# Attention's ScalarE loop written out, and a block's sums copied out by VectorE

## The reference

```python
q = (x_norm @ Wq + bq).reshape(B, S, H, hd).transpose(0, 2, 1, 3)
k = (x_norm @ Wk + bk).reshape(B, S, H, hd).transpose(0, 2, 1, 3)
v = (x_norm @ Wv + bv).reshape(B, S, H, hd).transpose(0, 2, 1, 3)
q = apply_rope(q)
k = apply_rope(k)
q = q * (1.0 / jnp.sqrt(jnp.float32(hd)))
scores = jnp.einsum('bhqd,bhkd->bhqk', q, k)
attn = jax.nn.softmax(scores, axis=-1)
out = jnp.einsum('bhqk,bhkd->bhqd', attn, v)
```

## Time and profile before

| what | value |
|---|---|
| time, median of 3 runs | 4466.51 us (4465.53 to 4467.92) |
| the profiled execution's own time | 4463.72 us |
| its span in the trace | 4462.0 us |
| TensorE busy | 93% of the span |
| VectorE busy | 70% |
| ScalarE busy | 60% |
| attention, blocks 1 to 30 | about 805 to 3308 us of the span |

### The profile page before, as it was taken

One profiled execution on the slowest core, in us unless ns is written; L12 is line 12 of the kernel. 1 busy time (PEld: TensorE's weight loads), 2 busy tenths in 40 slices (PEclk: granted clock), 3 DMA queues, 4 the chain that ended last, 5 costly groups with the idle time before them and its releaser, 6 DMA issues. The chain is left out here.

```text
span 4462.0 us, 71502 instructions
## 1 busy us (share of the span) xinstructions
PE 4160.7 (93%) x23748; PEld 1788.7 (40%) x23748; DVE 3137.1 (70%) x4158; ACT 2665.3 (60%) x5113; POOL 374.6 (8%) x444
## 2 busy tenths in 40 slices
PE   6988637999999999999999999999998899999999
PEld 4666401222222222222222222222225788876666
DVE  6877596999999999999999999999950011132332
ACT  4555304778777778778778778778784222222122
POOL 0222355000000000000000000000001000011110
PEclk8999758999999999999999999999999999999999
DMA  4232393000004000004000000000004755532221
GB/s 149 76 104 90 113 152 116 6 4 4 6 4 73 12 4 4 6 4 72 14 4 4 6 4 4 6 4 4 6 4 161 230 193 195 198 100 73 64 60 40
DMA packets 206165, 264.69 MB, mean 59 GB/s; under 512 B 24880, under 2 KB 169520, under 8 KB 204240
## 3 DMA queue, kind: packets, MB, share of 16 engines
q1 hardware_dynamic: 193872, 228.98, 17.8%
q0 software_dynamic: 11904, 31.10, 2.4%
HBM read 184.76 MB, written 74.97 MB: 58 GB/s over the span
## 5 line engine op out<-in xcount | busy, mean ns | idle before, releaser
L1172 ACT ACTIVATE a_PT<-a_PS 128x512 f32<-128x512 f32 x4096 | 2119.2, 603 | 687.6 <-PE a_PS L1046 608.3
L1253 DVE TENSOR_REDUCE a_MX<-a_PS 128x2 f32<-128x1024 f32 x1062 | 1290.6, 1221 | 149.0 <-PE a_PS L1031 136.0
L1259 DVE TENSOR_REDUCE a_MX<-a_PS 128x1 f32<-128x512 f32 x1972 | 1266.7, 684 | 66.2 <-PE a_PS L1031 45.6
L1046 PE MATMUL a_PS<-a_QS,a_KS 128*128 128x512 bf16 x4096 | 1075.5, 383 | 24.2 <-ACT a_PT L1172 9.5
L1056 PE MATMUL a_OT<-a_PT,a_VG 128*32 128x512 f32 x8192 | 1095.2, 607 | 0.9 <-ACT a_PT L1172 0.8
L1031 PE MATMUL a_PS<-a_KS,a_QS 64*128 64x512 bf16 x4096 | 731.5, 393 | 111.5 <-ACT a_PT L1172 48.2
L1031 PEld LDWEIGHTS a_PS<-a_KS,a_QS 64*128 64x128 bf16 x4096 | 172.5, 93 | 1179.6 <-ACT a_PT L1172 639.7
L1046 PEld LDWEIGHTS a_PS<-a_QS,a_KS 128*128 128x128 bf16 x4096 | 314.1, 97 | 624.6 <-DVE a_MX L1253 281.3
L1444 ACT ACTIVATE e_hT<-e_up,e_BF 128x256 f32<-128x256 f32 x312 | 148.2, 475 | 413.3 <-PE e_up L1397 413.2
L1397 PE MATMUL e_up<-e_xT,e_WF 128*128 128x256 f32 x1248 | 324.7, 383 | 0.8 <-DVE e_xT L1454 0.8
L1406 PE MATMUL e_dn<-e_WP,e_hT 128*128 128x256 f32 x1248 | 322.0, 381 | 0.0
(11 more groups left out here) (222 smaller groups left out, 2783.4 us busy)
## 6 DMA issues: line engine op xcount, KB each, us to landing
e_WF<-Wfc SPq DMA_DIRECT2D x39, 1024.0 KB, 5.0
e_WP<-Wproj SPq DMA_DIRECT2D x39, 1024.0 KB, 7.0
a_QS<-scr_qparts SPq DMA_DIRECT2D x384, 32.0 KB, 9.5
a_KS<-scr_kparts SPq DMA_DIRECT2D x48, 256.0 KB, 13.3
scr_xs<-f_zero SPq DMA_DIRECT2D x1, 9984.0 KB, 33.2
e_XS<-scr_xs SPq DMA_DIRECT2D x39, 256.0 KB, 2.7
scr_ys<-e_Y SPq DMA_DIRECT2D x39, 256.0 KB, 2.1
f_X<-x SPq DMA_DIRECT2D x16, 512.0 KB, 4.7
```

Source lines behind the costliest of these rows:

```text
L1046: T.matmul(score_bank(c), KS[j][:, h, u * P:(u + 1) * P], QS[j][:, bass.ds((b * HG + h) * BLK, BLK)], start=True, stop=True).then_inc(S["q ...
L1172: nc.scalar.activation(PT[:, c % RING, :], score_bank(c), ACT.Exp, scale=SOFT_SCALE).then_inc(S["exp_done"], 1)
L1253: V.tensor_reduce(MX[n % 2][:, :, x], PS[:, banks[0]:banks[0] + SIDES, :], AX.X, ALU.max).then_inc(S["mp_free"], SIDES)
L1259: V.reduce_max(MX[n % 2][:, side, x:x + 1], PS[:, banks[side], :], AX.X).then_inc(S["mp_free"], 1)
```

## The change

ScalarE's `act.Fori` over the blocks becomes a Python loop, so its 31 passes stand one after the other in the stream, with constants for the counts that its waits compare with. The copy of `OT` to `OS` goes from ScalarE to VectorE: a new function `copy_out(n)` with the same two waits, called at the start of VectorE's block n+1, before pair 0, and once at the very end. The first increment of `o_copied`, which stands for the copy of a block that doesn't exist, moves along.

```diff
@@ nc.scalar of attention @@
             act.sem_inc(S["av_done"], KT)
-            act.sem_inc(S["o_copied"], 1)
...
                 if more:
                     for c in range(HG):
                         exp(n + 1, c)
-                act.wait_ge(S["av_done"], (n + 2) * KT)
-                act.wait_ge(S["att_store"], n * 16 + 1 + 16)
-                nc.scalar.copy(OS[:], OT[:]).then_inc(S["o_copied"], 1)
 
             for c in range(HG):
                 exp(0, c)
-            with act.Fori(0, NG * NB - 1) as n:
+            for n in range(NG * NB - 1):
                 one_block(n, True)
             one_block(NG * NB - 1, False)
@@ nc.vector of attention @@
             c = Chain(dve, S["chain"])
+            dve.sem_inc(S["o_copied"], 1)
...
+            def copy_out(n):
+
+                dve.wait_ge(S["av_done"], (n + 2) * KT)
+                dve.wait_ge(S["att_store"], n * 16 + 1 + 16)
+                V.tensor_copy(OS[:], OT[:]).then_inc(S["o_copied"], 1)
+
             def one_block(n, more1, more2):
                 e = first_event(n)
+                if n:
+                    copy_out(n - 1)
                 for x in range(PAIRS):
...
             for n in range(blocks):
                 one_block(n, n + 1 < blocks, n + 2 < blocks)
+            copy_out(blocks - 1)
```

## The result

The changed kernel takes 4424.9 us (median of 4, 4413.6 to 4428.0), the kernel before 4466.0 beside it: a ratio of 0.9904, interval 0.9885 to 0.9923. It was compared on three more occasions: 0.9920 (0.9906 to 0.9933), 0.9914 (0.9901 to 0.9926) and 0.9924 (0.9911 to 0.9938). By the medians it gains 41, 36, 38 and 36 us. The forecast was 33 us, 4433.8 us, in a range of 4426 to 4450.

A forecast was written before the change was run, and what follows sets the result against it. TensorE was taken as the bound, idle mainly at 30 block boundaries behind ScalarE's branch back. Removing 1.46 us and adding 0.37 for the copy, 30 times, gave 32.7 us less: 4433.8 us from 4466.5, range 4426 to 4450.

The forecast's parts named there:

- The stall and its cause: ScalarE's loop end: the branch back forces an instruction fetch, and TensorE waits 1.32 us for an exponential, 30 times.
- The 1.46 us of a boundary: Between blocks: period 83.63 us against 82.17 without a stall; writing the loop out removes it 30 times, 43.8 us.
- The copy's cost: Start of VectorE's block: the copy delays reductions 0.52 us, 0.15 absorbed, costing 0.37 us in each of 30 blocks.
- the overlap: VectorE: operations of 0.68 us start 0.60 us apart, so the next starts before the one before is done.
- The prediction's reading of the Trainium skill: VectorE: no start until the previous pipe is empty; 0.71 us delay, 0.56 us cost, total gain 27 us; not followed.
- The sum over the blocks: Boundaries of blocks 1 to 30: 30 x (1.46 - 0.37) = 32.7 us less.
- The copy on ScalarE: gain: Taking the 0.62 us copy off ScalarE gains nothing, since ScalarE has slack in a step.
- "some us" for block 0: Block 0, where GpSimd's scatter disturbs every engine: some us allowed within the forecast's own spread of 4428 to 4442.
- the range: Whole kernel: 4426 to 4450 us, meant to take in most of the costly-copy rival at 4450 us (chance 0.14).
- the register instructions: Between ScalarE's exponentials: removing them gains nothing, because TensorE doesn't wait for ScalarE inside a block.

The follow-up runs named there:

- e6: Kernel of before with two blocks in a pass of ScalarE's loop, 14 branches back instead of 30, copies still on ScalarE: 4416.5 us, ratio 0.9950.
- e1: Changed kernel with the copy of OT left on ScalarE, so only the loop is written out: 4413.9 us, ratio 0.9896.
- e5: Changed kernel with ScalarE's loop kept and a bare wait on ScalarE where the copy was: 4439.7 us, ratio 0.9997.
- e8: Changed kernel with each block's sums copied twice on VectorE, first into a tile nobody reads: 4427.3 us, ratio 0.9972.
- g3: Kernel of before with ScalarE's block 0 written out and blocks 1 to 30 in the loop: 4438.4 us, ratio 0.9995.
- g4: Kernel of before with ScalarE's loop written out except block 0, which stands in a loop of a single pass: 4395.2 us, ratio 0.9893.
- e2: Changed kernel with ScalarE's loop back, so only the copy is moved to VectorE: 4431.8 us, ratio 0.9930.
- f1: Kernel of before, unchanged, run again as first of four combinations of the change's two parts: 4459.8 us, ratio 1.0003.
- e7: Kernel of before, loop and ScalarE's copy kept, each pass cut 8 exponentials behind the copy: 4405.8 us, ratio 0.9919.

## Why the prediction missed

**The stall and its cause: right.** The gap belongs to the branch back and not to the `weigh` that the profile names. `e6` has stalls only at branches, `e1` has none, and `e5` brings them back by a wait ahead of the branch. The 1.46 us of a boundary were measured as 83.63 - 82.16 = 1.47.

**The copy's cost: right.** 0.37 us were forecast and 82.55 - 82.16 = 0.39 measured, and 0.38 of it lies in the five scores where the prediction looked for it. That a longer delay of the reductions would pass one to one isn't shown, since in `e8` the `weigh` waited for the copy itself. The copy started 1.14 us behind a reduction of 1.23, and the next operation 0.60 behind a copy of 0.68, so the overlap holds here. The prediction's reading of the Trainium skill (VectorE: DVE Perf Modes, section The DRAIN you can't avoid) would have made the cost 0.56. That reading took one sentence of the section alone; the same section says that a next operation that isn't held, as it calls it, starts earlier, and with that the trace agrees.

**The sum over the blocks: right.** From block 0's copy to block 30's it is 2507.0 us before and 2474.1 after, 32.9 less; 32.7 were forecast.

**"The copy on ScalarE: gain": wrong on its own, though not in the sum.** I gave the move nothing, since ScalarE has slack in a step. The copy's time does cost nothing, but its wait held the branch back by about 1.2 us, just enough to bring the fetch into TensorE's way. Moving the copy alone brings a block to 82.61 us against 82.55 with both parts, so in blocks 1 to 30 either part brings nearly all of the gain, and both together hardly more than one. Over the whole execution that doesn't hold: by the medians the copy alone gained 28 and 27 us, both parts 36 and 38 beside it, and the loop alone 46 and 48. What I called the price of a branch is the price of a branch taken late. `e5` shows it by a bare wait.

**Outside blocks 1 to 30: the step that failed.** The sum gave everything but the 30 boundaries nothing, with "some us" for block 0 inside the range, and said that the register instructions were worth nothing. In the profiled pair the spans differ by 40.8 us: 3.1 before attention's first sums, 3.3 in block 0, 32.9 from its copy to block 30's, and 1.5 behind that.

Of these, only block 0's part repeats. Where before takes some 4460 us, six profiles with ScalarE's loop and six with it written out have the first sums at 688.7 and 688.3 us by their means, and the rest behind block 30's copy lasts 1151.7 and 1152.5. Block 0 is 5.9 us shorter when written out, with hardly any overlap between the two sixes. So the term that was mis-sized is block 0's, and the other 4.6 us of the pair are, by the same profiles, chance of two executions.

By the medians the changed kernel gained 3 to 5 us beyond the blocks' 33 in three comparisons and 8 in the first, and the copy alone 4 and 5 us less than its blocks account for. The interval of such a comparison is some 6 us to either side, and 8 in the first, so each by itself tells little.

On the occasions where block 0 takes some 91 us instead of 107 to 113, the means of three and two profiles are 1.4 us apart, and one of the three (93.7) makes that. So the extra gain goes with the larger disturbance, as far as these profiles tell. Which part of the loop is exposed to it, its register instructions or the branch into it, stays open: `g3` and `g4` were to tell, but they ran on an occasion without the effect. That without the scatter the medians are 37 us apart, where the blocks account for 34, isn't explained either; executions of one kernel there differ by 9 to 10 us.

The rest of the miss is the range. The runs that I saw before lay within 2.4 us, and the same kernel later spread over 17 on one occasion (4451 to 4468). The stages outside attention vary by several us between executions, which the lower bound left out.

## What to carry to other kernels

Here a hardware loop's branch back put 2.6 to 2.9 us between it and ScalarE's next exponential; whether that cost time depended on how far the sequencer was ahead of its engine when it took the branch. So look at what the last instructions of a body wait for: a late wait there exposed the fetch. Cutting the pass at another place brought 36 us and taking the wait out 27 to 28, where writing the loop out brought 45 to 48. When a change has two parts, run each alone: here the second part cost 0.39 us a block, and the better kernel, 4412 to 4414 us, is the one with the loop written out and the copy left on ScalarE.

## What the runs showed of the hardware

- From the first branch back to the next exponential it is 2.6 to 2.9 us in the eleven profiles with a loop of many passes: 2.6 before (branch 803.3, exponential 805.92), 2.7 in `e2` (799.0 and 801.66), and most in `f1` (800.1 and 803.02).

```profile
805.92 0.60 ACT L1172 ACTIVATE a_PT<-a_PS 128x512 f32<-128x512 f32 x1 [1.90 <-PE a_OT L1056]
```

```profile
801.66 1.57 ACT L1171 ACTIVATE a_PT<-a_PS 128x512 f32<-128x512 f32 x3 [1.24 <-PE a_PS L1046]
```

- Behind a branch ScalarE stood idle for 5.0 us while the packets of the queue with a later group's loads took 100.8% of the DMA engines' time (`e7`). Written out it had no such gap at the same loads: its longest wait in attention was 1.0 us in the changed kernel and 0.7 in `e1`.
- The register instructions of a loop's body cost TensorE nothing outside block 0: blocks without a branch take 82.06 us in the loop (`e6`) and 82.16 written out (`e1`).
- The queue of instructions moved 1.75 MB in 214 packets before and 1.01 MB in 123 after, so the written-out form needs less traffic here. The 91 packets are three for each of the 31 passes. That the body carries register instructions, and is fetched again in every pass, would explain them; no run tests it alone.
